# Dots of gathered rows with the softmax probability as a scale, and one silu per group of rows

## What is computed

```python
h = act(einsum('btd,cd->btc', hidden_states, W_up) + b_up)
h = einsum('btc,pc->btp', h, W_down) + b_down          # 256 numbers per token
...
sc, pk = lax.top_k(all_scores, K_PER_HEAD)
indices = take_along_axis(all_indices, pk, axis=-1)
de = down_embed[indices]
ue = up_embed[indices]
z = einsum('btd,bthkd->bthk', h, de)                   # the dots
z = act(z * softmax(sc, axis=-1))                      # act is silu
out = einsum('bthk,bthkd->btd', z, ue)                 # the weighing
```

## Time and profile before

| what | us |
|---|---|
| median of 3 runs | 3163.76 |
| lowest and highest | 3161.43, 3163.99 |
| span of the profiled execution | 3636.9 |

### The profile page before, as it was taken

One profiled execution on the slowest core, in us unless ns is written; L12 is line 12 of the kernel. 1 busy time (PEld: TensorE's weight loads), 2 busy tenths in 40 slices (PEclk: granted clock), 3 DMA queues, 4 the chain that ended last, 5 costly groups with the idle time before them and its releaser, 6 DMA issues.

```text
span 3636.9 us, 45017 instructions
## 1 busy us (share of the span) xinstructions
PE 2994.1 (82%) x12032; PEld 1872.2 (51%) x12032; DVE 2792.9 (77%) x10168; ACT 1976.8 (54%) x6257; POOL 2061.1 (57%) x2056
## 2 busy tenths in 40 slices
PE   8887888888888888888888788888888888888853
PEld 4555545555545555554555554555554555554431
DVE  3577878787887778887878787877888777787866
ACT  3455565555565555566555556555555555556522
POOL 0155655556655556656555655555666555666555
PEclk9899989989999899899998999999999999998876
DMA  7167777777877777777777777767877766777777
GB/s 265 58 201 239 255 236 228 229 240 252 260 238 236 226 233 261 249 241 248 236 232 239 248 235 239 235 225 240 265 245 254 234 226 220 254 241 246 234 233 246
DMA packets 189855, 856.77 MB, mean 236 GB/s; under 512 B 36192, under 2 KB 39392, under 8 KB 189088
## 3 DMA queue, kind: packets, MB, share of 16 engines
q0 software_dynamic: 163840, 805.44, 67.9%
q1 hardware_dynamic: 19104, 34.87, 2.7%
q10 hardware_dynamic: 6656, 13.60, 1.0%
HBM read 845.38 MB, written 8.39 MB: 235 GB/s over the span
## 4 chain that ended last, share of the span: by engine, by line
PE 53%; issue 11%; DVE 9%; POOL 8%; DMA 8%; ACT 6%; another core or an unknown queue 5%; DVEq 0%; SPq 0%; ACTq 0%; POOLq 0%
PE bank L464 13%; PE bank L501 8%; POOL ring L276 8%; DMA ring<-embed,idx 8%; PE bank L339 6%; PE bank L359 6%; PE bank L442 5%; DVE bank L1136 4%; PE bank L474 3%; PE bank L489 3%; PE bank L368 3%; ACT xc L680 2%; DVE ring L1122 2%; PE bank L376 1%
## 5 line engine op out<-in xcount | busy, mean ns | idle before, releaser
L276 POOL DMA_INDIRECT ring<-embed,idx x2048 | 2059.8, 1006 | 1561.0 <-issue 534.7
L1136 DVE SCALAR_TENSOR_TENSOR bank<-ring,coef,bank 128x512 f32<-128x512 f32 x1312 | 982.7, 749 | 48.0 <-issue 16.9
L1122 DVE SCALAR_TENSOR_TENSOR ring<-ring,hcur 128x256 f32<-128x256 f32 x2048 | 815.7, 418 | 249.4 <-DMA ring<-embed,idx 224.1
L501 PE MATMUL bank<-ring,diag_c 128*128 128x512 f32 x1344 | 697.5, 650 | 83.1 <-issue 50.2
L646 ACT ACTIVATE coef<-prob,zp 128x1 f32<-128x1 f32 x2048 | 455.2, 289 | 523.5 <-DVE ring L1122 305.7
L464 PE MATMUL bank<-zs,w_up 128*128 128x128 f32 x4096 | 569.3, 302 | 186.4 <-ACT zs L761 107.1
L464 PEld LDWEIGHTS bank<-zs,w_up 128*128 128x128 f32 x4096 | 548.0, 217 | 243.9 <-ACT zs L761 134.1
L501 PEld LDWEIGHTS bank<-ring,diag_c 128*128 128x128 f32 x1344 | 258.2, 206 | 340.2 <-issue 276.0
L767 ACT ACTIVATE seg<-bank,bup 128x128 f32<-128x128 f32 x512 | 146.1, 368 | 493.2 <-remote 318.6
L967 DVE SCALAR_TENSOR_TENSOR xc<-raw,taps,xc 128x128 f32<-128x128 f32 x960 | 264.7, 341 | 155.3 <-ACT xc L680 97.8
L474 PE MATMUL bank<-w_down,seg 128*128 128x256 f32 x1024 | 270.9, 413 | 58.7 <-issue 50.7
(11 more groups left out here) (144 smaller groups left out, 3689.6 us busy)
## 6 DMA issues: line engine op xcount, KB each, us to landing
ring<-embed,idx POOLq DMA_INDIRECT x2048
ring<-uT SPq DMA_DIRECT2D x4, 2048.0 KB, 14.3
ut<-uT SPq DMA_DIRECT2D x32, 256.0 KB
zs<-u SPq DMA_DIRECT2D x32, 256.0 KB
out<-acc SPq DMA_DIRECT2D x32, 256.0 KB
w_up<-W_upT ACTq DMA_DIRECT2D x1, 4096.0 KB, 12.8
w_in<-W_in ACTq DMA_DIRECT2D x1, 2560.0 KB, 17.4
w_in<-W_in ACTq DMA_DIRECT2D x1, 2048.0 KB, 21.9
```

The source lines that it names most:

```text
L276: pool.indirect_dma_start(out=ring[:, k % RING, :], out_offset=None, in_=embed, in_offset=bass.IndirectOffsetOnAxis(ap=idx[:, half, k:k + ...
L501: m = pe.matmul(bank[SUM][:, :], diag_c[:, (len(PE_ROWS) * t + n) % DIAGS, :], ring[:, k % RING, DP:ROW], start=(n == 0), stop=(n == len(P ...
L1122: m = dve.scalar_tensor_tensor(out=ring[:, k % RING, 0:DP], in0=ring[:, k % RING, 0:DP], scalar=1.0, in1=hcur[:, :], op0=ALU.mult, op1=ALU ...
L1136: dve.scalar_tensor_tensor(out=total if n == len(DVE_ROWS) - 1 else running[:, :], in0=ring[:, k % RING, DP:ROW], scalar=coef[:, k:k + 1], ...
```

## The change

Silu of (probability times dot) stays. What moves is the product with the probability. Before, ScalarE made it inside each silu, which therefore needed one instruction per row, since the scale is one number per partition. Now VectorE makes it inside the dot: the new instruction gives `out = (in0 * in1) * scale`, with `scale` the column of `prob`, and the sum of `out` from 0.0 on. `zp` then holds the product, and one silu over the columns of a group gives all its coefficients. The wait for the probabilities (`soft_ok`) at group 0 is dropped on ScalarE; on VectorE the same wait stands before group 0 already, and stays.

```diff
             def coefs(t, g):
 
-                if g == 0:
-                    act.wait_ge(soft_ok, 4 * t + 4)
                 act.wait_ge(dot_ok, NGRP * t + g + 1)
-                for k in range(FIRST[g], FIRST[g + 1]):
-                    m = act.activation(coef[:, k:k + 1], prob_v[:, k:k + 1], ACT.Silu, scale=zp[:, k:k + 1])
-                m.then_inc(coef_ok, 1)
+                act.activation(coef[:, FIRST[g]:FIRST[g + 1]], zp[:, FIRST[g]:FIRST[g + 1]], ACT.Silu).then_inc(coef_ok, 1)
...
             def dot(t, k, last):
 
                 dve.wait_ge(row_in[k % RING], 16 * (uses(k) * t + k // RING + 1))
-                m = dve.scalar_tensor_tensor(out=ring[:, k % RING, 0:DP], in0=ring[:, k % RING, 0:DP], scalar=1.0,
-                                             in1=hcur[:, :], op0=ALU.mult, op1=ALU.mult, accum_out=zp[:, k:k + 1])
+                m = dve.tensor_tensor_reduce(out=ring[:, k % RING, 0:DP], in0=ring[:, k % RING, 0:DP], in1=hcur[:, :],
+                                             scale=prob_v[:, k:k + 1], scalar=0.0, op0=ALU.mult, op1=ALU.add,
+                                             accum_out=zp[:, k:k + 1])
```

## The result

| | median us | lowest to highest | ratio to before, 95% interval |
|---|---|---|---|
| kernel before | 3162.6 | 3150.8 to 3164.0 | |
| changed kernel | 3223.8 | 3218.1 to 3230.6 | 1.0203 (1.0182 to 1.0224) |

What follows compares the result with a forecast made beforehand. The prediction took VectorE to set the pace of the plain run. Dots +100.4 us less 4.7 and 16.7 hidden, silus -11.8 and -10.7, gave +56.5 us on 3163.8: 3220.3 us (+1.8%), range 3140 to 3275.

Steps and rivals of the forecast that it cites:

- VectorE sets the pace: Whole tiles in a plain run: VectorE busy 94% of 92 us, with some 6 us of waiting per tile.
- the sign of 89.5 us a tile: Profile after the change: VectorE's busy time per tile should read 89.5 us and not 86.4.
- The read scalar costs 49 ns: VectorE's dots: reading prob per partition instead of constant 1.0 adds 49 ns to each of 2048, +100.4 us.
- The new instruction costs nothing on top: VectorE's dots: the new kind of instruction adds nothing beyond the read scalar; a dot takes 467 ns, not 418.
- 21.4 us hidden beside the waits: Dot growth covered by VectorE's waits: 4.7 us in group 5, 16.7 us in groups 18 to 21.
- The silus bring 22.5 us: ScalarE's silus, 2048 becoming 704: gains of 11.8 us at group 4 and 10.7 us at coefficient waits.
- the loop at group 4: Three-engine chain from a dot through silus, diagonals and projection copy to the convolution: 0.38 us saved a tile, -11.8 us.
- 10.7 us at the coefficients: VectorE's weighing waits 21.4 us in all for coefficients; half was taken as gained by faster silus, -10.7 us.
- A: Silus and coefficient waits: the silus win, faster; with the scalar free of charge 3141.3 us; chance 20%.
- B: VectorE's dots: nothing is hidden, since waits for gathered rows vanish in the plain run; 3264.2 us; chance 14%.
- C: VectorE's dots: the new instruction is dear, +119 ns a dot; 3333.0 us; chance 8%.
- D: TensorE and GpSimd set the pace more than thought; dots' growth and gain land in waits; 3163.8 us; chance 14%.

Runs made afterwards that it cites:

- the stand-in: Kernel before with the new product-and-sum dot instruction, its scale a constant 1.0, one silu per row as before: 3161.3 us, ratio 1.0017.
- the dots alone: Changed kernel with one silu per row again, each reading its scale from a column of ones: 3226.6 us, ratio 1.0222.
- the silus alone: Kernel before with one silu per group, old dots, the product with the probability left out: 3153.5 us, ratio 1.0000.
- the filling: Unread TensorE products before the transpose of h: three per tile in the changed kernel, 3202.4 us; two with one silu per group, old dots, no probability product, 3133.5 us.
- the hidden place: Kernel before with a read scalar in only 14 dots a tile, those of groups 5 and 18 to 21: 3161.7 us, ratio 1.0005.

## Why the prediction was right, point by point

**VectorE sets the pace: right, with a limit.** The tiles take 96.0 us of which VectorE works 89.6, and dots that are lengthened in an open place reach the time in full. The tile of the kernel before was put at 92 us for a plain run, of which VectorE would work 86.4. In the stand-in, over 28 tiles, it is 2615.6 / 28 = 93.4, of which VectorE works 2401.8 / 28 = 85.8:

```profile
319.30:2934.90 2615.60, 2406.45 (x10388) 1525.27 (x10388) 2401.83 (x8849) 1717.53 (x5461) 1807.79 (x1792) 0.97 0.84 279
```

So the sign of 89.5 us a tile came true at 89.6 partly by luck: the base was 0.6 us too high and the growth 0.7 too small. Another sign fits too: TensorE waits longer for VectorE, at L482 125.5 us against 45.2 in the stand-in, at L432 84.9 against 78.5, though about half of the first belongs to the silus (83.6 with the dots alone). But two rows moved to TensorE did not bring what VectorE's pace alone promised.

**The read scalar costs 49 ns: right in kind, too small.** It is 60 ns (417 to 477). The pair of rows that gave 49 had 128 columns where the dot has 256, and no accumulator; which of the two makes the difference was not tried. The mis-sized term is 2048 x 49 = 100.4 us; by busy time it is 118.6.

**The new instruction costs nothing on top: right**, 417 ns with a constant.

**21.4 us hidden beside the waits: right in place, too small in size.** The 14 dots named cost nothing. In all 38.3 us were hidden by the two profiles, and 54 by the medians. So the dots' half came out at 80.3 us in the spans against the 79.0 of the sum, and in the medians at 65 against the stand-in and 70 against the kernel before: the two errors nearly cancel.

**The silus bring 22.5 us: wrong.** They brought 0 (-7 to +7) alone, and between the changed kernel and the dots alone 1.0203 against 1.0222, 6 us and within the noise. The first term of it, -11.8 us through the loop at group 4, did come, but was given back: the convolution's wait fell by 12.2 us, and in the silus alone by 8.0 against the stand-in. (TensorE's wait for the copy at L668, 2.61 us in the earlier trace rows, is at most 0.6 us with the dots alone. The loop is there, but it is less tight than that row looked.) In the plain kernels the second, 10.7 us at the coefficients, was not there to win: in none of the later traces does VectorE's weighing wait for a coefficient, and the 21.4 us of the earlier trace rows belonged to the disturbed execution. And the step that failed most is one that the sum lacked: what becomes of an engine that is now early. TensorE stood idle longer before h, was granted the lower clock just behind, and held up VectorE's search by 16.6 us more; the filling shows that this is what it cost.

**The total** of +56.5 us against the measured +61 thus rests on two errors of opposite sign: the dots' half was put 9 to 14 us too high against the medians, and the silus' half promised 16 to 22 us that did not come. The side and the cause are right; the agreement to 4 us is partly luck.

**The rivals.** A fell with the 60 ns. B's 100 us (nothing hidden) fell with the hidden place. C fell with the new dot and a constant. D (absorbed) is what happened to the silus' half.

**The profile's own length.** The prediction held the holes for a part of the profile alone and added to the median. That was needed: against 3636.9 the changed kernel's profile even looks 11% faster.

## What to carry to other kernels

Before work is moved from a half-idle engine to the tightest one, price the operand and not only the instruction: here a per-partition scalar instead of a constant cost 60 ns each time, 14% of a dot, and it was paid 2048 times, while 1344 instructions saved on ScalarE gave nothing that could be measured. Ask of every dot or step which wait follows it; in this kernel 14 of 64 were free and 14 others cost all they were worth. And where an engine becomes early, look at what its idle time does to the next thing it must deliver.

## What the runs showed of the hardware

- A read scalar adds 60 ns to a VectorE product with 256 columns and an accumulator (417 to 477 ns with the new instruction, 418 to 478 with the old). Nearly all of it shows in the pace: VectorE's busy time grows by 118.6 us, 58 ns a dot.
- A product-and-sum instruction of three steps (product, scale, running sum) costs what a product with accumulator costs: 417 ns.
- One silu of 1 to 4 columns without a read scalar takes 187 to 205 ns. ScalarE: Activation LUTs, section What ACT_TABLE_LOAD costs (the Trainium skill), puts it at 186 ns plus 0.833 ns a column, and 93 more with a read scalar, so about 187 and 280 ns for one column (estimates from that page). The trace agrees for one column, 187 ns, and nearly with a read scalar, 286 ns with the dots alone; with 2 to 4 columns it has 202 to 205 ns, some 15 more than the page gives.
- TensorE, idle for 4.0 us or more before h, took longer than 3.60 us for the eight products of the key scores in 30 of 31 tiles of the changed kernel; in the tile shown they took 4.81 us, in a stretch with a granted clock of 0.71. After 1.9 to 2.0 us of idle time they took 3.60 us in 15 of 16 tiles of the dots alone; between these, after 2.6 to 3.1 us, in 16 of 28 tiles of the silus alone. Three useless products in each gap took 21 us off the kernel.
